# A transformer block with routed experts: choosing by least denominators on two engines, identity products in TensorE's pauses, and row maxima ahead of weight loads

## What is computed

```python
x = L0_attn_x                                 # (16, 256, 128), float32
xn = layernorm(x)
qkv = xn @ qkv_w.T + qkv_b                    # 16 heads of 8
attn = softmax(q @ k.T * 8 ** -0.5) @ v       # within each batch of 256 tokens
a = attn @ proj_w.T + proj_b
probs = sigmoid(xn @ W_router)                # 4096 tokens, 8 experts
topk_probs, topk_idx = top_k(probs, 2)
topk_probs = topk_probs / (sum(topk_probs) + 1e-6)
f = relu(xn @ W_sh_up) ** 2 @ W_sh_down       # shared expert
for e in the two experts of a token:
    f += weight_e * (relu(xn @ W_up[e]) ** 2 @ W_down[e])
out = x + a + f
```

## Time and profile before

| | us |
|---|---|
| three runs | 446.98, 448.91, 451.05 |
| median of them | 448.91 |
| profiled execution, whole | 452.23 |
| its span, from the first to the last instruction | 450.1 |
| TensorE busy | 427.7 (95%) |
| VectorE busy | 334.3 (74%) |
| ScalarE busy | 293.2 (65%) |
| GpSimd busy | 241.3 (54%) |
| mean granted clock of TensorE | 0.975 |

### The profile page before, as it was taken

One profiled execution on the slowest core, in us unless ns is written; L12 is line 12 of the kernel. 1 busy time (PEld: TensorE's weight loads), 2 busy tenths in 40 slices (PEclk: granted clock), 3 DMA queues, 4 the chain that ended last, 5 costly groups with the idle time before them and its releaser, 6 DMA issues.

```text
span 450.1 us, 12543 instructions
## 1 busy us (share of the span) xinstructions
PE 427.7 (95%) x4347; PEld 341.4 (76%) x4348; DVE 334.3 (74%) x625; ACT 293.2 (65%) x517; POOL 241.3 (54%) x358
## 2 busy tenths in 40 slices
PE   8989869999999999998999999999998999999996
PEld 7977726666666666665899999999998666666664
DVE  7786795888898888888666666666664788888723
ACT  1451645687678768877666766666664876876782
POOL 6064000766666555663277777677887556733320
PEclk9998965999999999999999999999999999999999
DMA  8384101054235435324455455554541452553120
GB/s 227 102 372 170 53 32 50 31 167 155 67 109 166 128 90 200 115 66 132 118 156 163 149 151 164 153 148 132 149 138 43 135 155 75 182 165 103 43 61 23
DMA packets 56322, 56.72 MB, mean 126 GB/s; under 512 B 6514, under 2 KB 46196, under 8 KB 55764
## 3 DMA queue, kind: packets, MB, share of 16 engines
q1 hardware_dynamic: 51060, 41.61, 31.3%
q0 software_dynamic: 4544, 9.35, 6.3%
q10 hardware_dynamic: 672, 5.15, 2.7%
HBM read 26.65 MB, written 16.59 MB: 96 GB/s over the span
## 4 chain that ended last, share of the span: by engine, by line
PE 84%; DVE 9%; issue 2%; DMA 2%; ACT 1%; SPq 1%; POOL 0%; DVEq 0%; POOLq 0%; ACTq 0%
PE pbank L1465 15%; PE obank L1320 13%; PE sbank L1345 12%; PE fbank L1263 7%; PE fbank L1151 4%; PE fbank L1152 3%; PE fbank L1153 3%; DVE maxes L1011 3%; PE wbank L1292 2%; PE tbank L1151 2%; PE pbank L1151 2%; PE tbank L1153 2%; PE tbank L1152 2%; PE sbank L1457 2%; PE obank L1179 2%
## 5 line engine op out<-in xcount | busy, mean ns | idle before, releaser
L1011 DVE TENSOR_REDUCE maxes<-sbank 128x4 f32<-128x1024 f32 x128 | 156.8, 1225 | 44.1 <-PE sbank L1345 39.4
L765 ACT ACTIVATE probs<-tbank 128x1024 f32<-128x1024 f32 x128 | 130.8, 1022 | 66.1 <-PE tbank L1350 64.4
L572 POOL DMA_INDIRECT answers<-gathered,block_rows x78 | 80.4, 1030 | 38.4 <-ACT gathered L817 22.7
L541 POOL DMA_INDIRECT tagged<-X,place_of x64 | 63.1, 985 | 33.5 <-PE tbank L1350 21.7
L1465 PE MATMUL pbank<-down_w,probs 128*128 x624 | 76.2, 275 | 1.4 <-ACT gathered L817 1.4
L1345 PEld LDWEIGHTS sbank<-k_bands,q_bands 31*128 31x128 f32 x512 | 39.8, 189 | 45.8 <-DVE maxes L1011 35.0
L1345 PE MATMUL sbank<-k_bands,q_bands 31*128 31x256 f32 x512 | 65.9, 334 | 8.8 <-DVE maxes L1011 7.6
L1465 PEld LDWEIGHTS pbank<-down_w,probs 128*128 128x128 f32 x624 | 72.7, 192 | 1.6 <-issue 1.6
L1320 PE MATMUL obank<-probs,v_ones 128*32 128x256 f32 x1024 | 70.9, 396 | 0.0
L1350 PE MATMUL tbank<-q_bands,k_bands 32*128 32x256 f32 x512 | 65.7, 335 | 0.3 <-ACT probs L765 0.3
L1118 DVE TENSOR_TENSOR block_lo<-block_w,block_hi 128x512 fp32r<-128x512 f32 x39 | 27.0, 692 | 41.4 <-ACT block_hi L798 41.3
(11 more groups left out here) (193 smaller groups left out, 901.7 us busy)
## 6 DMA issues: line engine op xcount, KB each, us to landing
block_w<-in_w_up SPq DMA_DIRECT2D x39, 256.0 KB, 2.7
q_bands<-part_hi SPq DMA_DIRECT2D x32, 128.0 KB
k_bands<-part_hi SPq DMA_DIRECT2D x32, 128.0 KB
tagged<-q_bands ACTq DMA_DIRECT2D x1, 4096.0 KB, 12.0
gathered<-answers SPq DMA_DIRECT2D x16, 256.0 KB, 4.0
gathered<-tagged SPq DMA_DIRECT2D x30, 129.0 KB, 2.2
q_bands<-part_lo SPq DMA_DIRECT2D x16, 128.0 KB
k_bands<-part_lo SPq DMA_DIRECT2D x16, 128.0 KB
```

The source lines that it names most:

```text
L541: pool.indirect_dma_start(out=tagged, out_offset=bass.IndirectOffsetOnAxis(ap=place_of[:, k, tile:tile + 1], axis=0), in_=X[:, tile, :], i ...
L572: pool.indirect_dma_start(out=answers, out_offset=bass.IndirectOffsetOnAxis(ap=block_rows[:, (p - 1) % 4, k:k + 1], axis=0), in_=ys[:, (p ...
L765: nc.scalar.activation(probs[:, j % 4, :], tbank[:], ACT.Exp, scale=SCALE).then_inc(exps_ready, 1)
L1011: nc.vector.tensor_reduce(maxes[:, g // 2, :, 2 * pair:2 * pair + 2, g % 2].rearrange("p t q -> p q t"), sbank[:].rearrange("p (q t k) -> ...
```

## The change

1. **The choice.** Sigmoid's value is one over a denominator, so the largest probability has the least denominator. Before, ScalarE adds 1 to the exponentials and VectorE takes the reciprocal of all 128 x 256; now VectorE adds 1 (and cuts at `FAR`), the choice goes by minima, a chosen entry is masked by adding `GONE`, and only the two chosen denominators of a token are inverted, in batch 3.
2. **Who does it.** GpSimd multiplies by ranks (`rank_best`), adds the two choices (`both_chosen`), makes the ranks by an iota in place of VectorE's eight small fills, and does the running sum of tile counts (`expert_starts`). Each has a semaphore to and from VectorE (`best_ready`, `ranked`, `tiles_counted`, `expert_starts_ready`).
3. **Where.** All steps of `choose` and `place` on VectorE stand behind `row_maxima` of their slot, and also behind `low_qk`, `hidden1` and `keep_values`, ahead of `normalise(b, 0)`. They have fewer slots (tables).
4. **Identity products** (`LAST_FILL`): 3 in slots (-1, 2) and (-1, 6), and in batch 0 two, two, six, two and six in slots 3 to 7, the latter into `fbank` once ScalarE has read the logits.
5. **Counts** go into `wbank`. The up products of batch 0 wait for their copy no longer, `turn` of slot (1, 2) does.
6. **SyncE**: `maxima(b, 1)` is issued ahead of the residual and the down weights, which move to the start of the next `body`; late stores and gathers thereby no longer stand behind the wait for `batch_added`.

```diff
+CHOOSE = {(0, 3): 0, (0, 4): 1, (0, 5): 2, (0, 6): 3, (3, 0): 4, (3, 1): 5, (3, 3): 6, (3, 5): 7, (3, 6): 8}
+PLACE = {(1, 2): 0, (2, 2): 1, (3, 2): 2, (4, 2): 3}
+FAR, GONE = 1e38, 2e38
+LAST_FILL = {(-1, 2): 3, (-1, 6): 3, (0, 3): 2, (0, 4): 2, (0, 5): 6, (0, 6): 2, (0, 7): 6}
...
             def body(b):
                 if has_values(b):
                     maxima(b, 1)
+                    if b != ROUTED_AT + 1:
+                        wait(sp, batch_added, b - 1)
+                        residual(b)
+                if b in (2, 3, 5, 6):
+                    if b == 5:
+                        sp.wait_ge(places_ready, 2)
+                    for e in {2: range(2), 3: range(2, 4), 5: range(4, 6), 6: range(6, 8)}[b]:
+                        sp.dma_start(down_w[:, e + 1], w_down[e].rearrange("(c p) d -> p c d", p=P)).then_inc(down_loaded, 16)
...
                 if has_maxima(b):
                     maxima(b + 1, 0)
-                    if b != ROUTED_AT:
-                        wait(sp, batch_added, b)
-                        residual(b + 1)
...
+            def rank_best(k):
+                pool.wait_ge(best_ready, 2 * k + 1)
+                nc.gpsimd.tensor_tensor(table(3), table(3), rank[:].unsqueeze(1).to_broadcast([P, TILES, E]),
+                                        ALU.mult).then_inc(ranked, 1)
+            def both_chosen():
+                pool.wait_ge(best_ready, 4)
+                nc.gpsimd.tensor_tensor(chosen[:], table(1), table(2), ALU.add).then_inc(chosen_ready, 1)
+            def expert_starts():
+                link(nc.gpsimd.memset(tile_counts[:, 4, :], 0.0))
+                pool.wait_ge(tiles_counted, 1)
+                for c in range(3):
+                    step = 1 << c
+                    link(nc.gpsimd.tensor_copy(tile_counts[:, c + 1, 0:step], tile_counts[:, c, 0:step]))
+                    link(nc.gpsimd.tensor_tensor(tile_counts[:, c + 1, step:], tile_counts[:, c, step:], tile_counts[:, c, 0:E - step], ALU.add))
...
                 def best(k, src):
-                    link(nc.vector.tensor_reduce(chosen_rows[:, k, :], src, AX_X, ALU.max))
-                    link(nc.vector.tensor_tensor(work, src, bc(chosen_rows[:, k, :]), ALU.is_equal))
-                    link(nc.vector.tensor_tensor(work, work, wt, ALU.mult))
+                    link(nc.vector.tensor_reduce(chosen_rows[:, k, :], src, AX_X, ALU.min))
+                    nc.vector.tensor_tensor(work, src, bc(chosen_rows[:, k, :]), ALU.is_equal).then_inc(best_ready, 1)
 
                 def first(k):
+                    dve.wait_ge(ranked, k + 1)
                     link(nc.vector.tensor_reduce(chosen_rows[:, 2, :], work, AX_X, ALU.max))
-                    link(nc.vector.tensor_tensor(table(1 + k), work, bc(chosen_rows[:, 2, :]), ALU.is_equal))
+                    nc.vector.tensor_tensor(table(1 + k), work, bc(chosen_rows[:, 2, :]), ALU.is_equal).then_inc(best_ready, 1)
 
                 if j == 0:
-                    for e in range(E):
-                        nc.vector.memset(rank[:, e:e + 1], float(E - e))
-                    dve.wait_ge(exp_logits_ready, 2)
+                    dve.wait_ge(exp_logits_ready, 1)
+                    link(nc.vector.tensor_scalar(p, p, 1.0, FAR, ALU.add, ALU.min))
+                    best(0, p)
                 if j == 1:
-                    link(nc.vector.reciprocal(p, p))
+                    first(0)
+                    dve.wait_ge(best_ready, 2)
+                    link(nc.vector.scalar_tensor_tensor(out=rest, in0=table(1), scalar=GONE, in1=p, op0=ALU.mult, op1=ALU.add))
...
                     if j == 5 and N:
                         keep_values(b + 1)
+                    if (b, j) in CHOOSE:
+                        choose(CHOOSE[b, j])
+                    if (b, j) in PLACE:
+                        place(PLACE[b, j])
                     if j == 6 and A:
                         normalise(b, 0)
...
+                    if (b, j) in LAST_FILL:
+                        if b == 0:
+                            pe.wait_ge(exp_logits_ready, 1)
+                        fill(LAST_FILL[b, j], obank if b < 0 else fbank)
```

More of the change, by code:

```diff
@@ L701, in routing @@
                                          scale=-1.0).then_inc(exp_logits_ready, 1)
-                    act.wait_ge(exp_logits_ready, 1)
-                    nc.scalar.activation(table(0), table(0), ACT.Identity, bias=1.0).then_inc(exp_logits_ready, 1)
                 if (b, j) == (1, 0):
@@ L947, in choose @@
+                    link(nc.vector.scalar_tensor_tensor(out=rest, in0=table(1), scalar=GONE, in1=p, op0=ALU.mult, op1=ALU.add))
                 if j == 2:
-                    best(0, p)
+                    best(1, rest)
                 if j == 3:
-                    first(0)
+                    first(1)
                 if j == 4:
-                    link(nc.vector.scalar_tensor_tensor(out=rest, in0=table(1), scalar=-2.0, in1=p, op0=ALU.mult, op1=ALU.add))
+                    link(nc.vector.reciprocal(chosen_rows[:, 0:2, :], chosen_rows[:, 0:2, :]))
@@ L954, in choose @@
                 if j == 5:
-                    best(1, rest)
-                if j == 6:
-                    first(1)
-                    nc.vector.tensor_tensor(chosen[:], table(1), table(2), ALU.add).then_inc(chosen_ready, 1)
-                if j == 7:
                     dve.wait_ge(places_ready, 2)
                     link(nc.vector.tensor_tensor(chosen_rows[:, 2, :], chosen_rows[:, 0, :], chosen_rows[:, 1, :], ALU.add))
+                if j == 6:
+                    link(nc.vector.tensor_scalar(chosen_rows[:, 2, :], chosen_rows[:, 2, :], 1e-6, None, ALU.add))
@@ L1083, in body @@
                         prepare(TURN[b, j])
-                    for k in CHOOSE.get((b, j), ()):
-                        choose(k)
-                    if (b, j) in PLACE:
-                        place(PLACE[b, j])
                     if (b, j) == (-1, 1):
@@ L1290, in turn @@
                 pe.wait_ge(out_kept, 2 * c + n + 1)
+                if (c, n) == (0, 1):
+                    pe.wait_ge(counts_kept, 1)
                 for t in range(TT):
```

81 lines of the change are left out of this document (38 added, 43 removed).

## The result

The changed kernel takes **447.05 us** (median of 14 launches, 444.82 to 451.32). The ratio of the two is **0.9914 [0.9885, 0.9944]**, 0.9% or 3.9 us faster. The ratios in this document leave out the slow launches, those over 1.5% above the fastest of their kernel, and the medians do not, which is why the two medians lie further apart, by 5.7 us. The forecast of 444.9 us was 2.15 us too low; the measured time lies within the stated range (441.8 to 448.6), but above the bounds of the forecast's own case (443.3 to 446.3). Profiled: 447.52 us, span 445.6, against 452.23 and 450.1.

What follows compares the result with a forecast made beforehand. Batch 0 was taken as bound by VectorE, batch 1 up to 79.4 by TensorE at half speed. Profiled: -1.6 - 2.2 - 4.0 + 2.2 = -5.6 us; median, without -1.6: 448.91 - 4.0 = 444.9 us, range 441.8 to 448.6.

Steps and rivals of the forecast that it cites:

- The clock: Sign of being right: no 0.50 in the granted clock between 47 and 90 us.
- rivals 1 and 2: 1: clock still falls, batch 1 slow, 448.4, chance 0.25; 2: identity products delay score products, 452.5, chance 0.06.
- Before batch 0: Six identity products in two TensorE pauses keep the clock up ahead of batch 0: -1.6 us, otherwise 0.
- Batch 0: Shorter choice on VectorE lets batch 1 start at about 65.6 and not 67.76: -2.2 us.
- Batch 1: At full clock batch 1 takes 16.9 us against 20.9: -4.0 us, some 3.5 of it from the clock.
- Batches 3 and 4: Steps moved behind `part_lo`, where VectorE has no slack, add 0.45 us net in batch 3 and 0.78 in batch 4.
- the forecast of 0.94: Batch 2: a memset and three comparisons moved behind `part_lo`, where there is no slack, add 0.94 us.
- Late batches: From batch 10 on, GpSimd's row additions run at other moments: -0.8 or +0.8 us per collision with VectorE, taken as 0.
- SyncE: Row maxima issued ahead of the weights, bias rows behind them; no TensorE pause waits for those maxima: 0.
- Behind it on GpSimd wait its own `place` and the first scatter, which nobody awaits before the end of batch 2; it still starts earlier than before: Batch 1: GpSimd work behind the 2.3 us running sums of tile counts, given no cost.
- the term of batches 2 to 4: Steps moved behind `part_lo` on VectorE cost +2.2 us over batches 2 to 4, bounds 0 to +2.6.
- The gain of 4.0 us: Forecast for the median execution, supposed to have the first slow stretch at full speed already: 448.91 to 444.9 us.

Runs made afterwards that it cites:

- e1: Changed kernel without the added identity products in the slots of batches -1 and 0; 451.41 us, 0.9999 of the kernel before.
- e5: Changed kernel with a second buffer for batch 1's sum and the steps of batches 2 to 4 ahead of the row maxima again; 442.96 us, ratio 0.9830.
- e7: Changed kernel with SyncE's order of the kernel before (residual and expert weights ahead of the second half's maxima); 448.00 us, ratio 0.9927.
- e4: Changed kernel with a buffer of its own for batch 1's sum, so its add no longer waits for scatters; 447.22 us, ratio 0.9921.
- e10: Changed kernel with twelve unread one-column writes on GpSimd ahead of the choice; 446.74 us, ratio 0.9890.
- e12: Changed kernel with two unread one-column writes on GpSimd ahead of the choice; 446.02 us, ratio 0.9899.
- e2: Kernel before with the changed kernel's identity products alone; 449.65 us, ratio 0.9990.
- e8: Kernel before with the identity products alone, eight instead of two in slot 3 of batch 0; 448.23 us, ratio 0.9927.
- e6: Changed kernel with an unread VectorE reciprocal of the whole 128x256 table added in slot 4 of batch 0; 451.14 us, ratio 0.9991.
- e13: Changed kernel with the steps of batches 2 to 4 ahead of the row maxima and twelve unread GpSimd writes; 446.00 us, ratio 0.9896.
- e3: Changed kernel with the steps of batches 2 to 4 ahead of the row maxima again; 447.76 us, ratio 0.9931.
- e9: Changed kernel with the second buffer and the steps of batches 1 to 4 ahead of the row maxima; 442.73 us, ratio 0.9810.
- e11: Changed kernel with the two rank products and the sum of both tables back on VectorE; 445.84 us, ratio 0.9879.

## Why the prediction was off

**Right, by its own steps.** *The clock*: no 0.50 between 47 and 90 us, nor anywhere before the last few us; rivals 1 and 2 did not come. *Before batch 0*: -1.5 us (-1.6), but the cause is open: e1 has 18.88 us there without the six products, with its pause of 0.74 us and the clock full. *Batch 0*, between score products as the prediction cut it: 45.63 to 63.80 is 18.17 us, -2.4 (-2.2); the add that I put at 0.40 took 0.28, the masking 0.43 as supposed. *Batch 1* likewise: 16.94 us against the forecast of 16.9, -3.9. *Batches 3 and 4*: 0.9 and 0.8 us lost (0.45 and 0.78), by the pauses of 0.77 and 0.64 us for row maxima behind the moved steps; e5 gives them back. In batch 2 the same pause is 0.89 us, where row maxima and scores had been in step: the forecast of 0.94 was right as far as it went. *Late batches*: the one pause of 0.8 us became three of 0.30, 0.19 and 0.27; 0, as supposed. *SyncE*: 0, as far as e7 can tell.

**The step that failed: "Behind it on GpSimd wait its own `place` and the first scatter, which nobody awaits before the end of batch 2; it still starts earlier than before".** It does start earlier, at 80.87 and not 84.64 us, and the last scatter of batch 1's tiles too. But `add_batch(1)` stands at the end of batch 2, and without the wait that end would have come forward by 7.0 us (from 104.59 to 81.28 + 16.28, with e4's batch 2), the last scatter by 4.5 (from 100.10 to 95.59). I had looked at when the chain starts and not at how long it is: 15.7 us. Batch 2 lost 2.7 us and not 0.94; the term of batches 2 to 4 was +4.3 and not +2.2. e4 shows it: with that wait gone alone, batch 2 is 1.8 us shorter. e10 and e12 show that the start counted as well: without GpSimd's idle 2.58 us, for which the prediction had nothing, batch 2 is 1.7 us shorter.

**The sum.** For the profiled execution I had -5.6 us; its span went from 450.1 to 445.6, -4.5. The difference is the 2.1 us too little for batches 2 to 4, less 0.8 us that the stage of routed blocks gave (153.16 to 152.39 us), for which I had nothing, and less some 0.2 over the other stages. Those 0.8 us are one wait at the end of the stage: TensorE waited 1.40 us for ScalarE's last `gathered` before and 0.56 after. e2 and e8 have them too (152.3 and 152.4) with SyncE's old order, and e1 (153.5) doesn't, so they come neither from the new order nor from the new choice. They go with the products; why stays open.

**The level.** The gain of 4.0 us that I put on record agrees with the 3.9 of the ratio, and that is luck. I got to 4.0 by taking 1.6 us off the sum, on the supposition that the median launch has its first slow stretch at full speed already. No run bears that out: 96 more launches of the kernel before have a mean granted clock of 0.977 in the median, and the profiled execution, with all its slow stretches, 0.975. The 1.6 us taken off for a wrong reason happened to stand in for the 2.1 us of the failed step less the 0.8 of the routed stage. The starting point was off besides: the three launches in the table, with a median of 448.91, were short ones. Of the 96, those that a ratio compares (83) have a median of 451.0, 2.1 us higher, and this is the 2.15 us by which 444.9 was too low.

Launches differ with their clock. Of the 96, those at 0.972 to 0.977 (36) have a median of 452.1 us, those at 0.984 to 0.989 (9) one of 448.3. The changed kernel's launches have 0.996 in the median. Lines through all launches of before, changed and e1 give 2.5, 2.8 and 3.3 us for each 0.01, so by an estimate from them the 0.019 between the two kernels are worth 4.7 to 6.2 us, more than the kernels differ by; batches 2 to 4 take part of it back.

**What stays open.** Why the clock falls behind one pause and not behind another: it held behind 1.92 us (e6), 1.79 (changed) and 2.00 (e13), and fell behind 1.67 (e2), 2.29 (e3), 1.58 (e7) and 1.99 (e1). My reading "each fall has a pause of 0.74 us or more ahead of it" stands in all profiled executions, up to their last 10 us; the reverse doesn't. What else separates e2, which gains nothing in the timed launches, from e8 is open too: six products in one slot are all the difference in code.

## What to carry over

When a change shortens the stretches ahead of a long serial chain on a slow engine, compare the chain's length, not only its start, with the time until its first waiter: a wait that was covered by slow code comes to light when the code gets fast. Take out each part by itself, and look at the parts' sum: here the kernel without the unread products in TensorE's pauses gains nothing (e1), those products alone gain as much as the whole change once the longest pause has enough of them (e8, but not e2), and a rewritten choice that shortens its own stretch by 2.5 us nets nothing until two small losses behind it (a buffer and the place of a few steps) are mended together. Compare kernels at the same clock: what separates these two in the timed launches goes mostly with how often the clock falls.

## What the runs showed of the hardware

- **GpSimd can stand idle where its program has nothing to wait for**, 2.4 to 2.65 us at one position of it (the profile names no releaser in seven of the eight executions, TensorE in e1), with two packets of a queue of kind "instruction" in that time. Two small operations added ahead left 0.68 us, moved the packet forward, and made the kernel's batch 2 1.7 us shorter.
- **An indirect scatter's landing varies.** VectorE was released 2.4 us (e3), 3.45 (changed) and 4.3 (e13) after the start of the eighth scatter.
- **TensorE can run at about half pace while the granted clock reads 1.00.** At the very start twelve matmuls of identity products took 2.93 us in the changed kernel's profiled execution and 1.60 in e5's, and the first maxima came at 27.3 us or 25.3; which of the two differs between profiled executions of kernels that start alike (27.3 in before, changed, e8, e9 and e10; 25.3 in e1 to e7, e12 and e13; 26.1 in e11). The Trainium skill (TensorE: Matmul & The Clock Gate, Part 1: The HAM clock gate) says that the number of slow products at the start of one and the same kernel varies from run to run; the traces agree. The timelines of TensorE, first the changed kernel's, then e5's:

```profile
8.55 2.93 PE L1203 MATMUL obank<-ident 128*128 128x128 f32 x12
```

```profile
7.59 1.60 PE L1207 MATMUL obank<-ident 128*128 128x128 f32 x12
```
